# Turning an item's tokens once: one transpose set feeds two copies, and every engine's order is laid anew

## The reference

```python
for i in range(DEPTH):
    x = attn_layer(shift_tokens(x), Wqkv[i], q_scale[i], k_scale[i], Wo[i]) + x
    x = ffn_layer(shift_tokens(x), ln_g[i], ln_b[i], W1[i], b1[i], W2[i], b2[i]) + x
```

## Time and profile before

| | |
|---|---|
| median of 3 runs | 3527.9 us (3526.22 to 3528.53) |
| profiled execution | 3527.28 us, its span 3525.5 us |
| PE busy | 3293.5 us (93%) |
| DVE busy | 2843.1 us (81%) |
| POOL busy | 2640.0 us (75%) |
| ACT busy | 1832.3 us (52%) |
| PEld busy | 1611.1 us (46%) |

### The profile page before, as it was taken

One profiled execution on the slowest core, in us unless ns is written; L12 is line 12 of the kernel. 1 busy time (PEld: TensorE's weight loads), 2 busy tenths in 40 slices (PEclk: granted clock), 3 DMA queues, 4 the chain that ended last, 5 costly groups with the idle time before them and its releaser, 6 DMA issues. The chain is left out here.

```text
span 3525.5 us, 69882 instructions
## 1 busy us (share of the span) xinstructions
PE 3293.5 (93%) x26940; PEld 1611.1 (46%) x26940; DVE 2843.1 (81%) x3289; ACT 1832.3 (52%) x2692; POOL 2640.0 (75%) x1918
## 2 busy tenths in 40 slices
PE   5788876899999999999999999999999999999986
PEld 3222222454555545454545455555555454545443
DVE  5788846888888888888888888888888888888862
ACT  2477772454545454555555555555454545455532
POOL 3133206998888888888888888888888888888850
PEclk7799998999999999999999999999999999999998
DMA  6232214333333323333323333333333233333211
GB/s 209 73 63 48 47 37 113 79 73 73 71 86 79 80 71 72 83 71 82 78 71 79 79 81 77 73 73 85 83 74 79 68 78 78 83 77 71 71 46 49
DMA packets 178233, 270.01 MB, mean 77 GB/s; under 512 B 42481, under 2 KB 67185, under 8 KB 176241
## 3 DMA queue, kind: packets, MB, share of 16 engines
q1 hardware_dynamic: 174160, 251.10, 29.6%
q10 hardware_dynamic: 3744, 14.43, 1.1%
HBM read 44.49 MB, written 19.55 MB: 18 GB/s over the span
## 5 line engine op out<-in xcount | busy, mean ns | idle before, releaser
L1084 DVE SCALAR_TENSOR_TENSOR ly_prod<-ly_pj_ps,ly_few,ly_tables 128x1024 f32<-128x1024 f32 x768 | 964.6, 1272 | 190.1 <-ACT ly_sq L1216 165.5
L1216 ACT ACTIVATE ly_sq<-ly_pj_ps 128x512 f32<-128x512 f32 x768 | 451.0, 601 | 745.8 <-PE ly_pj_ps L918 702.7
L918 PE MATMUL ly_pj_ps<-ly_xs,ly_wqk 128*128 128x512 f32 x1536 | 796.1, 616 | 35.2 <-DVE ly_prod L1084 22.5
L999 PE MATMUL ly_to_ps<-ly_u,ly_mvo 128*128 128x512 f32 x1536 | 720.6, 598 | 0.1
L1325 POOL TENSOR_TENSOR ly_sq<-ly_sq 128x512 f32<-128x512 f32 x384 | 491.6, 1280 | 220.0 <-ACT ly_sq L1216 219.8
L1247 ACT COPY ly_u<-ly_pair_ps 128x1024 f32<-128x1024 f32 x384 | 378.7, 1013 | 240.6 <-PE ly_pair_ps L987 240.6
L1329 POOL TENSOR_TENSOR ly_sx<-ly_sx,ly_smax 128x1024 f32<-128x1024 f32 x192 | 366.2, 1907 | 145.3 <-DVE ly_smax L1124 145.3
L918 PEld LDWEIGHTS ly_pj_ps<-ly_xs,ly_wqk 128*128 128x128 f32 x1536 | 269.2, 191 | 426.4 <-issue 291.5
L999 PEld LDWEIGHTS ly_to_ps<-ly_u,ly_mvo 128*128 128x128 f32 x1536 | 277.1, 190 | 287.2 <-issue 287.2
L987 PE MATMUL ly_pair_ps<-ly_pt,ly_xt 32*128 32x512 f32 x3072 | 385.3, 615 | 19.9 <-ACT ly_u L1247 13.0
L967 PE MATMUL ly_pair_ps<-ly_kbd,ly_qp 128*32 128x128 f32 x12288 | 374.7, 276 | 22.2 <-DMA ly_kbd<-ly_kr 18.9
(11 more groups left out here) (113 smaller groups left out, 4317.5 us busy)
## 6 DMA issues: line engine op xcount, KB each, us to landing
ly_qp<-ly_qr SPq DMA_DIRECT2D x768, 128.0 KB, 2.3
ly_kbd<-ly_kr SPq DMA_DIRECT2D x1536, 64.0 KB, 2.0
ga_parts_dram<-ga_parts SPq DMA_DIRECT2D x16, 384.0 KB, 2.3
ga_qs<-ga_parts_dram SPq DMA_DIRECT2D x96, 64.0 KB
ga_ks<-ga_parts_dram SPq DMA_DIRECT2D x96, 64.0 KB
ly_wqk<-in_wqk SPq DMA_DIRECT2D x24, 256.0 KB, 4.0
ly_mvo<-mvo_dram SPq DMA_DIRECT2D x6, 1024.0 KB, 6.4
mvo_dram<-ga_pt ACTq DMA_DIRECT2D x4, 1024.0 KB, 4.0
```

The lines of the kernel that those rows point to most:

```text
L918: pe.matmul(pj_ps[:, j % 2, :], wqk[:, g, j % TILES, :], xs[:, n % 2, WIN:], start=True, stop=True).then_inc(proj_ready.sem, 1)
L999: last = pe.matmul(to_ps[:], mvo[:, h, :], u[:, :, :, h, :].rearrange("p t c q -> p (t c) q"), start=(h == 0), stop=(h == LH - 1))
L1084: dve.scalar_tensor_tensor(prod[:, k], pj_ps[:, j % 2, :].unsqueeze(1).to_broadcast([P, 2, N]), gains[:, n // B, k:k + 1], tables[:, table ...
L1216: act.activation(sq[:, k, :], pj_ps[:, j % 2, :], ACT.Square).then_inc(sq_done.sem, 1)
```

## The change

`token_transposes` now turns each of the item's four blocks of 128 tokens once, into one bank of the slot, where before it did so twice, the second time for windows of `xs` that begin 32 tokens earlier, into the slot's other bank. `copy_tokens` then writes both versions from that bank: the item's own tokens in one copy over 128 partitions, the earlier ones in three copies of 32 partitions each that move down by 32 partitions, and a fourth of 32 partitions that also moves on by one block. The 32 rows in front of the first block stay zero and are set once at the start. `xt_done` counts five where it counted one. The longest copy is half of the old one.

All five orders are written anew. The items are renamed by one iteration on TensorE, ScalarE and VectorE (what was x_1 is x_0), which alone moves nothing.

```diff
-        xt_done = tally("xt_done", 1)
+        xt_done = tally("xt_done", 5)
...
             def token_transposes(n):
-                k = slot(("xt", n), xt_done, xt_done.at(n, 1))
-                for late in range(2):
-                    for t in range(T):
-                        at = t * P + WIN * late
-                        last = pe.transpose(pair_ps[:, k, late, t * P:(t + 1) * P], xs[:, n % 2, at:at + P], ident[:])
+                k = slot(("xt", n), xt_done, xt_done.at(n, 5))
+                for t in range(T):
+                    last = pe.transpose(pair_ps[:, k, 0, t * P:(t + 1) * P], xs[:, n % 2, WIN + t * P:WIN + (t + 1) * P], ident[:])
                 last.then_inc(xtr_ready.sem, 1)
...
             dve.memset(xs[:], 0.0).then_inc(xs_set, 1)
+            dve.memset(xt[0:32, 0, 0, :], 0.0).then_inc(xs_set, 1)
             dve.memset(kbd[:], 0.0).then_inc(kbd_set, 1)
...
-                act.copy(xt[:].rearrange("p l t c -> p l (t c)"), pair_ps[:, where["xt", n]]).then_inc(xt_done.sem, 1)
+                turned = pair_ps[:, where["xt", n], 0, :].rearrange("p (t c) -> p t c", t=T)
+                act.copy(xt[:, 1], turned).then_inc(xt_done.sem, 1)
+                for c in range(3):
+                    act.copy(xt[32 * c + 32:32 * c + 64, 0], turned[32 * c:32 * c + 32]).then_inc(xt_done.sem, 1)
+                act.copy(xt[0:32, 0, 1:T], turned[96:128, 0:T - 1]).then_inc(xt_done.sem, 1)
...
-                if x_1 is not None: square_sums(x_1, 3)
-                if x_5 is not None: down(x_5)
-                if x_2 is not None: token_transposes(x_2)
...
+                if x_4 is not None: down(x_4)
+                if x_1 is not None: scores(x_1, 3)
+                if x_0 is not None: square_sums(x_0, 3)
+                if x_1 is not None: token_transposes(x_1)
```

More of the change, by code:

```diff
@@ L813, in bodies @@
         def bodies(body):
-            for i in range(-1, ITEMS + 6):
-                body(i, known(i + 1), *(known(i - k) for k in range(7)))
+            for i in range(-1, ITEMS + 5):
+                body(i, known(i + 1), *(known(i - k) for k in range(6)))
         @block.sync
@@ new lines, in body @@
+            def body(i, x_ahead, x_0, x_1, x_2, x_3, x_4, x_5):
+                if x_0 is not None: project(x_0, 0, 1)
+                if x_3 is not None: combine(x_3, 2, 3, 4, 5)
+                if x_1 is not None: spread_norms(x_1, 0)
+                if x_3 is not None: combine(x_3, 6, 7)
+                if x_1 is not None: spread_norms(x_1, 1)
+                if x_3 is not None: combine(x_3, 8)
+                if x_0 is not None: project(x_0, 2)
+                if x_3 is not None: combine(x_3, 9)
+                if x_0 is not None: project(x_0, 3)
+                if x_3 is not None: combine(x_3, 10)
+                if x_0 is not None: project(x_0, 4)
+                if x_4 is not None: spread_rstd(x_4)
+                if x_3 is not None: combine(x_3, 11, 12, 13, 14)
+                if x_1 is not None: scores(x_1, 0)
+                if x_0 is not None: square_sums(x_0, 0)
+                if x_3 is not None: combine(x_3, 15)
+                if x_2 is not None: attend(x_2, 0)
+                if x_0 is not None: project(x_0, 5, 6)
+                if x_2 is not None: attend(x_2, 1)
+                if x_0 is not None: project(x_0, 7)
+                if x_1 is not None: scores(x_1, 1)
+                if x_4 is not None: up(x_4, 0)
+                if x_0 is not None: project(x_0, 8, 9); square_sums(x_0, 1)
+                if x_2 is not None: attend(x_2, 2)
+                if x_0 is not None: project(x_0, 10)
+                if x_1 is not None: spread_norms(x_1, 2)
+                if x_0 is not None: project(x_0, 11)
+                if x_1 is not None: spread_norms(x_1, 3)
+                if x_4 is not None: up(x_4, 1)
+                if x_3 is not None: centred(x_3)
+                if x_0 is not None: project(x_0, 12)
+                if x_2 is not None: attend(x_2, 3)
+                if x_0 is not None: square_sums(x_0, 2); project(x_0, 13)
+                if x_4 is not None: up(x_4, 2)
+                if x_1 is not None: scores(x_1, 2)
+                if x_0 is not None: project(x_0, 14, 15)
+                if x_4 is not None: down(x_4)
+                if x_1 is not None: scores(x_1, 3)
+                if x_0 is not None: square_sums(x_0, 3)
+                if x_1 is not None: token_transposes(x_1)
+                if x_0 is not None: sums_by_token(x_0)
+                if x_3 is not None: variance(x_3)
+                if x_2 is not None: combine(x_2, 0, 1)
```

219 lines of the change are left out of this document (88 added, 131 removed).

## The result

The changed kernel takes 3508.0 us (median of 9 runs, 3503.66 to 3518.77), the kernel before 3527.9 (9 runs, 3522.82 to 3531.52). The ratio of the mean times is 0.9948, 95% interval 0.9936 to 0.9959: about 0.5% or 18 us faster (the medians are 19.9 apart). The forecast was 3513, the range 3495 to 3538. In a later comparison the changed kernel took 3512.6 with a ratio of 0.9955 [0.9942, 0.9968].

The account below looks back on a forecast made before the run. TensorE was taken to bound the layers. Per item 59.4 us against 59.63, -10 over some 46 periods, with -5 for start and end, took 3527.3 to 3512 profiled, so 3513 as median; range 3495 to 3538.

Parts of the forecast that it names:

- Transposes, -0.43: TensorE's token transposes: four blocks less is half, 0.43 us less per item, called the one certain gain.
- Copies, nothing: ScalarE's five token copies, 0.5 us each, 2.5 in all: no cost, with cover of 1.3 us or more.
- Piece A 23.4: TensorE from token transposes to first `attend`: 23.4 us, before 23.83; includes -0.09 for tile 4 moving from before `attend`.
- B 13.28: TensorE from the first `attend` to the third: unchanged at 13.28 us.
- C 22.7: TensorE from the third `attend` to the next transposes: 22.7 us, before 22.52; +0.3 for a wait, -0.1 for tile shapes.
- The wait of the second `up`: TensorE between third `attend` and next transposes: `up` waits 0.3 us for VectorE to scale the keys of group 2.
- ScalarE's chain in C: `centred_squares`, table load, Exp, `take_u` 6 after the third `attend`: fits, ending at 12.1 us; third `up` wants it at 12.2.
- Rival 3: ScalarE's chain after the third `attend` is longer, as by a dearer table switch: if doubled, 3568 us; chance 0.15.
- rival 1: The counted TensorE waits don't come: -0.55 us per item, 3498 to 3503 us with start and end; chance 0.22.
- Start and end, -5: First and last items: fewer waits for `rotate` and for the last probabilities before `attend`, -5 us, bounds 0 and -10.
- 46 periods, -10: Some 46 full item periods at 59.4 us against 59.63, -0.2 each: -10 us.
- rival 2: Two or three thin TensorE margins become waits of 0.1 to 0.2 us: period 59.6 to 59.8, 3521 to 3535; chance 0.21.

Follow-up runs that it names:

- experiment 1: Kernel before with only the new transposes and copies: 3549.5 us, ratio 1.0074; changed kernel with the old transposes and copy: 3525.1 us, ratio 1.0015.
- experiment 2: Changed kernel with two or four more 32x512 ScalarE copies per item behind the five: 3508.9 us (ratio 0.9947) and 3560.8 us (1.0094).
- experiment 4: Changed kernel with one more 128x512 ScalarE copy per item just ahead of `take_u` 6: 3525.1 us, ratio 0.9990.
- experiment 3: Changed kernel with Relu in place of Gelu, so no table loads in the layers (it computes another gate): 3511.5 us, ratio 0.9950.

## Why the prediction was right

**Transposes, -0.43.** Right, a little high. The next matmul starts 0.49 after them in place of 0.87, which is 0.38; exchanged alone they are worth 0.41 (experiment 1).

**Copies, nothing.** Right: 1.18 us more is free, 2.40 us more costs 1.14 (experiment 2). That the cover is the 1.3 us of the prediction is luck: its 1.3 ran from the end of the copies to the end of `norms` and left out the 0.6 of the squares and the 1.14 by which `score_maxima` puts the product off. The size was low: 2.91 us in place of 2.5, since each of the first four copies starts 0.60 after the one before and not 0.50 as the squares do. It did not matter, because 1.3 us of cover is what is left after it.

**Piece A 23.4, B 13.28, C 22.7.** Measured 23.49, 13.28, 22.80. The two differences, 0.09 and 0.10, take three quarters of the gain per undisturbed item: 59.57 in place of 59.4, from 59.63. In A the 0.09 of tile 4 did not come. `combine` 15, now directly ahead of `attend`, takes 1.07 from start to start (1705.51 to 1706.58); before, it took 0.97:

```profile
1650.37 1.12 PE L999 MATMUL ly_to_ps<-ly_u,ly_mvo 128*128 128x512 f32 x2
```

The longer step went from tile 4 to it. In C the terms from start to start are `spread_norms` 3 with its wait 0.69 for 0.53, the second `up` 1.82 for 1.72, `centred` and tile 12 1.81 for 1.94, and the two `scores`, now apart, 3.66 for 3.52; this last 0.14 the prediction did not have. The wait of the second `up` came where it was forecast: some 0.25 (0.69 less the 0.44 of `spread_norms`), forecast 0.3.

**ScalarE's chain in C.** Right: `centred_squares` ends at 1728.54, the load takes it to 1729.84, the Exp and `take_u` 6 to 1731.80, and the third `up` follows at 1732.15. Tile 13 ahead of it takes 0.96 from start to start, as a tile beside a change of tile shape does in the earlier trace rows (0.95), so there is no wait. The margin of 0.1 was of the right size, somewhat low (0.17 to 0.28 by experiment 4). The Trainium skill (ScalarE: Activation LUTs, What ACT_TABLE_LOAD costs) gives 1283 ns for a load, which the rows have, and about 1380 ns of drain for each switch, which no row here shows: the idle time ahead of 181 loads is 3.2 us in all. Rival 3, which rested on a dearer switch, falls with experiment 3, and rival 1 with the wait of the second `up`.

**Start and end, -5.** The direction was right, the size too small: by the rows the fill gave 2.6 and the end 8.1. From the first `project` to the first transposes the three profiled runs in the old orders take 84.3 to 86.3 us, the ten in the new ones 80.9 to 83.8. Of the 8.1, 3.5 lie in the last iteration (52.13 in place of 55.59 from the 47th transposes to the 48th). The transposes are 0.38 of it, and two waits of TensorE are gone, here in its timeline before:

```profile
3371.21 1.06 PE L956 MATMUL ly_pair_ps<-ly_ident,ly_rnx 128*128 128x128 f32 x8 [1.25 <-DVE ly_sx L1117]
3413.80 1.96 PE L967 MATMUL ly_pair_ps<-ly_kbd,ly_qp 128*32 128x128 f32 x64 [1.80 <-DMA ly_kbd<-ly_kr]
```

The first is for `mask_scores` 3, which now stands ahead of `norms`; the second for the keys' DMA, at the `scores` 3 that stood directly behind `scores` 2. Another 2.2 lie ahead of the last item's `attend`, which comes 15.66 us after its transposes in place of 17.86: the wait of 1.76 that the forecast named is gone. 1.6 is one dip of the granted clock in the kernel before, told of below. The last 0.9 lie behind the last `down`, where nothing was changed. The forecast had seen only the 1.76. The size also holds luck: from the 47th transposes to the end the old orders took 160.1 to 162.7 us in their profiled runs, the new ones 154.6 to 159.4, and the 154.6 is the changed kernel's.

**46 periods, -10.** Here is the term that was mis-sized most. It measured -4.4, made of three parts: 0.07 less per undisturbed item, about -3; the uneven periods of before gone, about -8 (why they are gone is not shown); five boundaries of the changed kernel, +5 (the rest, about +1, lies in the first items). The step that the prediction left out is the uneven periods. It saw the 0.2 us of unevenness in the earlier trace rows and carried it along unchanged, and for the queries' DMA it allowed GpSimd a wait of up to 1 us at no cost without asking what else SyncE issues ahead of it at a layer's first item.

The sum, -15 by forecast, is -17.7 by the profile; 2.5 of this lies ahead of the changed part. The total was right in part by luck, because the errors cancel: the steady part was too large by 6, start and end too small by 6. The prediction named a period of 59.3 to 59.5 as a sign of being right, and 59.6 to 59.8 as rival 2. The undisturbed period is 59.57 and the mean of the 43 is 59.69: in the steady part the gain was mostly absorbed, as rival 2 says, and what brought the time down to 3508 is the start and the end. The other signs came: half the matmuls in L973, 91 and 90 loads, ScalarE 200 us busier (forecast some 190), and the wait of the second `up`.

## What to carry to other kernels

Two halves of a change can each bring nothing or a loss and be a gain together: when an operation becomes longer on an engine with idle time, what counts is what stands behind it in that engine's order, and past the cover, 1.3 us here, the whole delay is paid. Work out a margin as the time at which the result is wanted less the time at which it is there, and test it with dummy work of known length; two such runs bounded the cover here and gave what a delay beyond it costs. In a kernel that repeats one item many times read not one period but all of them: the items at which something else happens (a layer's weights) are where a queue's order shows. Moving one line of SyncE's order was worth 5 to 7 us by the periods, more than the whole change in the steady part (4.4). Read start and end of the kernel apart from the periods: here they gave the larger part of the gain.

## What the runs showed of the hardware

A ScalarE copy out of PSUM of 32 partitions and 512 columns takes 575 ns in the mean over 144, one of 128 partitions and 512 columns 585 over 48: four times the partitions cost 10 ns, so four narrow copies cost nearly as much as four wide ones. The lines of the changed kernel:

```profile
L1239 ACT COPY ly_xt<-ly_pair_ps 32x512 f32<-32x512 f32 x144 | 82.8, 575 | 3.5
L1237 ACT COPY ly_xt<-ly_pair_ps 128x512 f32<-128x512 f32 x48 | 28.1, 585 | 7.7 <-PE ly_pair_ps L973 6.6
```

The Trainium skill (ScalarE: Activation LUTs, What ACT_TABLE_LOAD costs) says that an ACTIVATE runs at one element per cycle and lane, whatever the function. The copies agree as far as this goes: the time follows the elements of one partition (the last narrow copy, of 384 columns, takes 473 ns) and hardly the number of partitions.

In the last items TensorE waits about 2 us at a time, and in some profiled runs the granted clock falls there. In the kernel before it is 0.83 between 3440 and 3450 us, a mean between the levels of 2.4 GHz (1.00) and 1.2 GHz, after waits of 1.76 and 2.10, and an `attend` of 2.00 us takes 3.59; the changed kernel has the same wait of 2.10, the clock stays at 1.00, and `attend` takes 2.00. The timelines of TensorE before and after:

```profile
3440.33 3.59 PE L987 MATMUL ly_pair_ps<-ly_pt,ly_xt 32*128 32x512 f32 x16 [2.10 <-ACT ly_u L1247]
```

```profile
3425.10 2.00 PE L984 MATMUL ly_pair_ps<-ly_pt,ly_xt 32*128 32x512 f32 x16 [2.10 <-ACT ly_u L1248]
```

It is worth 1.6 us here; with two more copies (experiment 2) the clock was 0.66 between 3370 and 3380 us and again between 3420 and 3430. The wait of 2.10 ahead of this `attend` (or 2.11) stands in all 13 profiled runs; in nine of them the `attend` behind it takes 2.61 to 3.70 us, in four, both runs of the changed kernel among them, 2.00. Why one run has it and the next not stays open.
